# A gated cross-attention kernel on one core: the context arrives in 32-row blocks that VectorE turns, and three engines' lists are reordered

## The reference, cut to what matters

```python
x = x + jnp.tanh(g_xattn[0]) * xattn(layernorm(x), ctx, ctx, mask, W_q, b_q, W_k, b_k, W_v, b_v, W_o, b_o)
x = x + jnp.tanh(g_ffn[0]) * ffn(layernorm(x), gate_w, w1, w2)
# xattn, x and ctx are (4, 512, 256); 16 heads of 16; windows of 64 queries that see
# their own and the previous 64 keys, causal:
q, k, v = query @ W_q.T + b_q, ctx @ W_k.T + b_k, ctx @ W_v.T + b_v
attn = softmax(where(causal & valid & mask, q k^T / 4, lowest)); out = (attn v) @ W_o.T + b_o
# ffn: top-1 router over 16 experts, 160 places each; gelu(tokens @ w1[e]) @ w2[e], weighted
```

## Time and profile before

| | |
|---|---|
| median of 3 runs | 324.27 us (322.58 to 327.51) |
| the profiled execution | 323.56 us, its span in the trace 321.8 us |
| busy, share of the span | PE 93%, DVE 61%, ACT 55%, POOL 51% |
| attention of four batches | to about 165 us |
| transition and experts | 165 us to the end |

### The profile page before, as it was taken

The page is one execution under the profiler, slowest core; times in us unless marked ns, Lnnn a source line. Parts: engine busy times, 40 slices in busy tenths (PEclk is TensorE's granted clock), DMA queues, the critical chain, the costliest instruction groups (busy, mean ns, idle before and its releaser), DMA issues.

```text
span 321.8 us, 8449 instructions
## 1 busy us (share of the span) xinstructions
PE 300.3 (93%) x2759; PEld 245.3 (76%) x2760; DVE 195.4 (61%) x950; ACT 177.1 (55%) x666; POOL 165.5 (51%) x201
## 2 busy tenths in 40 slices
PE   7869879999999999999899999999999999999994
PEld 3438746887758866777788788888988989898974
DVE  2888898898999879899974331423325161515133
ACT  3479999999999999999755111111110202111110
POOL 6379647789769974989857112131313121121222
PEclk9997999999999999999999999999999999999999
DMA  7921299017512290230324689598979797997900
GB/s 217 280 95 25 81 378 298 5 26 239 189 67 91 58 305 3 94 86 9 92 98 182 173 234 353 171 364 255 365 226 368 216 367 245 310 305 246 373 20 13
DMA packets 48471, 60.55 MB, mean 188 GB/s; under 512 B 14712, under 2 KB 41360, under 8 KB 46384
## 3 DMA queue, kind: packets, MB, share of 16 engines
q1 hardware_dynamic: 44976, 53.20, 51.6%
q0 software_dynamic: 2560, 6.25, 5.3%
q10 hardware_dynamic: 896, 0.61, 0.6%
HBM read 44.60 MB, written 14.19 MB: 183 GB/s over the span
## 4 chain that ended last, share of the span: by engine, by line
PE 50%; ACT 26%; DVE 9%; issue 6%; DMA 4%; SPq 3%; POOL 1%; POOLq 0%; DVEq 0%; ACTq 0%
ACT probs L714 18%; PE bank L1765 18%; PE bank L1790 14%; PE bank L1815 4%; PE bank L1426 3%; ACT probsT L727 3%; DVE probs L960 3%; DMA w<-in_L_ffn_w_dram 2%; ACT q_par L688 2%; SPq L331 2%; PE bank L1437 2%; PE bank L1539 2%; PE bank L1479 1%; DMA x_all<-in_x_dram 1%; PE bank L1501 1%
## 5 line engine op out<-in xcount | busy, mean ns | idle before, releaser
L714 ACT ACTIVATE probs<-probs,low 128x128 f32<-128x128 f32 x256 | 99.3, 404 | 2.2 <-DVE low L960 2.2
L535 POOL TENSOR_TENSOR probs<-probs,r_total 128x512 f32<-128x512 f32 x64 | 66.4, 1047 | 18.4 <-DVE r_total L969 18.0
L1765 PEld LDWEIGHTS bank<-xdT,w 128*128 128x128 f32 x480 | 66.5, 190 | 2.8 <-issue 2.2
L1765 PE MATMUL bank<-xdT,w 128*128 128x160 f32 x480 | 68.0, 300 | 0.6 <-issue 0.4
L960 DVE CUSTOM_DVE_ANT_0 probs<-bank,mask_now 128x128 f32<-128x128 f32 x256 | 57.2, 283 | 7.6 <-PE bank L1467 7.2
L714 ACT ACTIVATION_READ_ACCUMULATOR probs<-probs,low 128x1 f32 x256 | 52.4, 205 | 0.0
L884 ACT ACTIVATE w_raw<-bank 128x480 f32<-128x480 f32 (+1 forms) x24 | 12.6, 526 | 61.4 <-PE bank L1765 57.6
L639 POOL DMA_INDIRECT out_dram<-base,place x16 | 14.0, 875 | 59.0 <-DVE base L1325 38.2
L648 POOL DMA_INDIRECT out_dram<-base,place x16 | 15.7, 980 | 53.8 <-DVE place L1318 43.6
L884 ACT ACTIVATE x_all<-bank 128x480 f32<-128x480 f32 (+1 forms) x24 | 12.6, 527 | 53.2 <-PE bank L1765 53.2
L1335 DVE SCALAR_TENSOR_TENSOR base<-bank,base 128x256 f32<-128x256 f32 x15 | 7.2, 482 | 51.7 <-PE bank L1790 51.6
(11 more groups left out here) (148 smaller groups left out, 495.4 us busy)
## 6 DMA issues: line engine op xcount, KB each, us to landing
w<-in_L_ffn_w_dram SPq DMA_DIRECT2D x32, 1024.0 KB, 7.1
expert_queue<-empty_row SPq DMA_DIRECT2D x1, 5140.0 KB, 17.7
q_blocks<-expert_queue SPq DMA_DIRECT2D x62, 40.0 KB, 3.0
base<-expert_queue SPq DMA_DIRECT2D x16, 129.0 KB, 4.6
ctx_rows<-in_ctx_dram SPq DMA_DIRECT2D x4, 512.0 KB, 9.7
out_dram<-rows SPq DMA_DIRECT2D x4, 512.0 KB, 6.3
x_all<-in_x_dram SPq DMA_DIRECT2D x3, 512.0 KB, 7.7
v_shift<-v SPq DMA_DIRECT2D x12, 128.0 KB, 2.3
```

The costliest lines, as they stand in the source:

```text
L535: pool.tensor_tensor(probs[:, i % NP_], probs[:, i % NP_], r_total[:, i % NP_].unsqueeze(2).to_broadcast([P, PAIRS, 2 * WINDOW]), ALU.mult ...
L714: last = act.activation(probs[:, i % NP_, j], probs[:, i % NP_, j], ACT.Exp, scale=-1.0, bias=low[:, i % NP_, j:j + 1], accum_out=total[:, ...
L1765: last = pe.matmul(ps_hidden[m][:, c * CAP:(c + 1) * CAP], w1_sb[i % 2][:, k, f * P:(f + 1) * P], xdT[i % 2][:, k], start=(k == 0), stop=( ...
```

## The change

- The tile `ctx_rows` becomes `ctx_blocks`, of the same size. For batch 0 it is still loaded as rows (`load_first_ctx`) and turned by PE (`first_ctxT_of`).
- For batches 1 to 3 `load_ctx(n)` issues four transfers. Each takes a quarter of the columns (64 of them, 256 bytes) of all 512 rows, as 16 blocks of 32 rows, into 32 partitions. It waits for `ctxT_turned` instead of `ctxT_ready`, and stands at the end of SP's list of a batch instead of at its start (`load_ctx(1)` stands right ahead of the loop, as before in effect).
- DVE turns the blocks straight into `ctxT` with two STREAM_TRANSPOSE of 512 elements for each partition (`turn_ctx(b + 1, 0)` and `(b + 1, 1)`), behind `take_v(b, 1)`. `ctxT_of` on PE and `take_ctxT` on ACT are gone for these batches. `ctxT` now holds even columns in its first half and odd ones in its second, so `wT_of` turns W_k and W_v, and `first_ctxT_of` batch 0's context, with a column step of two.
- The lists of PE, ACT, DVE and POOL get a new order within each batch and in the last one. `turn_queued_xd`, the first turn of queued rows, moves from the start of the expert stage into the last batch, ahead of `rank_of(LAST - 1)`.

```diff
-        ctx_rows = sb("ctx_rows", [P, T, D])
+        ctx_blocks = sb("ctx_blocks", [P, S // BLOCK, KD * BLOCK])
+        first_ctx = ctx_blocks[:].rearrange("p s c -> p (s c)").rearrange("p (t d) -> p t d", d=D)
...
             def load_ctx(n):
-                if n > 0:
-                    sp.wait_ge(ctxT_ready, value(n - 1, 2, 2))
-                sp.dma_start(ctx_rows[:], ctx_in[n].rearrange("(t p) d -> p t d", p=P)).then_inc(ctx_in_s, 16)
+                if not 0 <= n < B:
+                    return
+                if n == 1:
+                    sp.wait_ge(ctxT_ready, 2)
+                else:
+                    sp.wait_ge(ctxT_turned, value(n - 2, 2, 2))
+                for j in range(P // BLOCK):
+                    sp.dma_start(ctx_blocks[j * BLOCK:(j + 1) * BLOCK],
+                                 ctx_in[n, :, j * KD * BLOCK:(j + 1) * KD * BLOCK].rearrange("(s r) c -> r s c", r=BLOCK)
+                                 ).then_inc(ctx_in_s, 16)
...
+            load_ctx(1)
             for b in range(B):
-                if b < LAST:
-                    load_ctx(b + 1)
                 shift_v(b, 0)
...
                 if b > 0:
                     store_x1(b - 1)
+                load_ctx(b + 2)
...
+            def turn_ctx(n, half):
+                if not 0 <= n < B:
+                    return
+                dve.wait_ge(ctx_in_s, 16 + 16 * (P // BLOCK) * n)
+
+                dve.wait_ge(v_ready, value(n - 1, 2, 2))
+                blocks = slice(half * (S // BLOCK // 2), (half + 1) * (S // BLOCK // 2))
+                dve.transpose(ctxT[:, :, half * (S // 2):(half + 1) * (S // 2)].rearrange("p k (s r) -> p s k r", r=BLOCK),
+                              ctx_blocks[:, blocks].rearrange("p s (r k) -> p s k r", k=KD)).then_inc(ctxT_turned, 1)
...
-                pe.wait_ge(ctxT_taken, value(n, 2, 2))
+                if n == 0:
+                    pe.wait_ge(ctxT_taken, 2)
+                else:
+                    pe.wait_ge(ctxT_turned, value(n - 1, 2, 2))
```

More of the change, by code:

```diff
@@ L348, in _ @@
             load_x(0, T // 2, T, x_in_late)
-            load_ctx(0)
+            load_first_ctx()
             for i, b in enumerate((b_q, b_k)):
@@ L603, in _ @@
             norm(LAST, 1)
+            x1_norm(LAST - 1, 0)
             scatter(LAST - 2, 2)
             norm(LAST, 2)
-            scatter(LAST - 2, 3)
             norm(LAST, 3)
             norm(LAST, 4)
-            x1_norm(LAST - 1, 0)
+            x1_norm(LAST - 1, 1)
+            scatter(LAST - 2, 3)
             norm(LAST, 5)
-            x1_norm(LAST - 1, 1)
-            x1_rstd_of(LAST - 1, 1)
             norm(LAST, 6)
@@ L615, in _ @@
             norm(LAST, 8)
+            x1_rstd_of(LAST - 1, 1)
+            norm(LAST, 9)
+            norm(LAST, 10)
             x1_norm(LAST - 1, 2)
-            norm(LAST, 9)
-            x1_norm(LAST - 1, 3)
-            norm(LAST, 10)
             norm(LAST, 11)
@@ L624, in _ @@
             norm(LAST, 15)
+            x1_norm(LAST - 1, 3)
             x1_rstd_of(LAST, 0)
             scatter(LAST - 1, 0)
+            scatter(LAST - 1, 1)
             x1_rstd_of(LAST, 1)
-            scatter(LAST - 1, 1)
             x1_rstd_of(LAST, 2)
@@ L690, in take_q @@
                 last.then_inc(q_taken, 1)
[L692 to L698, removed]
             def take_k(n, g, ps):
@@ L805, in _ @@
                 exp(b, 5)
-                take_probsT(b, 1)
                 exp(b, 6)
                 exp(b, 7)
+                take_probsT(b, 1)
                 take_xnT(b + 1, 0, ps_misc)
+                exp(b, 8)
                 take_probsT(b, 3)
+                exp(b, 9)
                 take_x1nT(b - 1, 0)
[L812 to L816, removed]
                 take_xnT(b + 1, 1, ps_misc)
@@ L1242, in _ @@
             low_of(LAST, 7)
+            take_v(LAST, 0, ps_misc)
             take_probsT(LAST, 0)
-            take_v(LAST, 0, ps_misc)
             r_total_of(LAST, 4)
@@ L1296, in turn_queued_xd @@
-            def turn_queued_xd():
-                dve.wait_ge(rows_in[0], 16 * (P // BLOCK))
-                turn_rows(0).then_inc(queued_turned, 1)
             def take_first_xd():
@@ L1370, in pair @@
                     take_y(e + 1, i + 1)
-            turn_queued_xd()
             take_first_xd()
@@ L1593, in _ @@
             for k in range(KD):
-                ctxT_of(0, k, bank[k])
+                first_ctxT_of(k, bank[k])
             keep_warm(bank[3], 3)
@@ L1620, in _ @@
                 probsT_of(b, 0)
-                probsT_of(b, 1)
                 scores(b, 2)
@@ L1636, in _ @@
                 v_of(b, 1, ps_misc)
+                probsT_of(b, 4)
+                probsT_of(b, 5)
+                pe.wait_ge(v_taken, value(b, 2, 2))
+                xnT_of(b + 1, 1, ps_misc)
+                scores(b, 3)
+                pe.wait_ge(xnT_taken, value(b + 1, 2, 2))
+                x1nT_or_gate(b - 1, ps_misc)
                 if first:
@@ L1659, in _ @@
                 q_of(b + 1, 0, ps_misc)
+                probsT_of(b, 7)
                 if not first:
@@ L1696, in _ @@
             probsT_of(LAST - 1, 15)
-            probsT_of(LAST, 0)
             pe.wait_ge(q_taken, value(LAST, 2, 2))
@@ L1701, in _ @@
             attend(LAST - 1, 3)
+            probsT_of(LAST, 0)
+            probsT_of(LAST, 1)
             scores(LAST, 2)
-            probsT_of(LAST, 1)
             probsT_of(LAST, 2)
```

177 lines of the change are left out of this document (88 added, 89 removed).

## The result

The changed kernel takes 325.34 us in the median of 10 runs (323.93 to 326.67); beside it, the kernel before took 323.41 us in the median of 10 (322.58 to 327.51). The ratio is 1.0051, with an interval of 1.0031 to 1.0071: half a per cent slower, which is 1.6 us (1.0 to 2.3). The interval is far narrower than the 2% that the prediction took as the least that could be told. Forecast was 1.0% less, and 325.34 lies above the upper bound of 324.4. The profiled execution took 325.34 us with a span of 323.5, against 323.56 and 321.8.

The account below looks back on a forecast made before the run. ACT was taken to bound the first stage. Copies -2.9, idle ahead of them -0.5, xnT1 wait +0.5, take_q waits -0.5 and last batch +0.2 gave -3.2 us: 324.27 to 321.1 us, range 317.6 to 324.4.

Parts of the forecast that it names:

- What bounds the kernel: First stage, 35 to 146 us: ACT is fullest, about 36 of each 37 us, with the other engines close behind.
- What goes: ACT loses six context copies, 2.9 us, and 0.5 us idle ahead of them; PE loses transposes, 2.6 us.
- What comes: DVE gets two turns a batch at 0.65 us, 3.9 in all (2.6 to 4.2), covered by its idle time.
- rival 3: DVE becomes the bound: the turns' full 3.9 us are added and ACT's saving is worth nothing, 328.2 us; chance 0.06.
- (5): New order: norm and DVE collide in ways the order shifts, each worth 0.9 us either way; taken as none.
- (1) to (4): New order: later take_v makes ACT wait 0.5 us at xnT1; later norms and POOL steps hidden; take_q waits shrink 0.5.
- (6): Batch 0's context transposes and those of W_k and W_v read with a step of two; taken as zero.
- (7): turn_queued_xd moves into the last batch, where DVE is nearly full: cost 0 to 0.44 us, taken 0.2.
- The loads: Four smaller context transfers a batch cost nothing, hidden by 19 us of cover on SP; bytes some 26% longer.
- rival 4: Context blocks arrive late and the turn waits; fourfold occupation, 31 us, makes shift_v 4.4 late: 325.5 us; chance 0.03.
- The marks: First take_q of batches 1 to 3 starts 1, 2 and 3 us earlier; expert stage unchanged in length.
- Rival 2: ACT, freed, waits for DVE's low or PE's take_q; only some 0.5 us come back, 323.8 us; chance 0.19.

Follow-up runs that it names:

- e4: Kernel before, with the mask set for batch 0 alone and router weights of batches 0 to 2 written by a reciprocal without their factor: 324.35 us, ratio 0.9992.
- e10: Kernel before, with GpSimd writing the finished mask instead of DVE's mask operation: 323.66 us, ratio 0.9997.
- e13: e9 with each of the six turns done a second time into a spare tile that nothing reads: 324.64 us, 1.0050 of the kernel before.
- e1: Kernel before with the context in blocks and the turns alone, all engines keeping their old lists: 324.48 us, ratio 1.0010.
- e2: Changed kernel with its new loop, but the last batch's lists and turn_queued_xd in the old order: 326.57 us, 1.0083 of the kernel before.
- e6: Changed kernel with the mask set once, for batch 0 alone: 322.88 us, 0.9967 of the kernel before.
- e8: Changed kernel with two mask buffers, the mask set behind the second turn, and ACT multiplying the weights of batches 0 and 1: 323.09 us, 0.9968 of the kernel before.
- e9: Changed kernel with GpSimd writing the finished mask into three buffers, no mask operation on DVE: 322.62 us, 0.9968 of the kernel before.
- e5: Changed kernel with router weights of batches 0 to 2 written by a reciprocal, without their factor: 325.33 us, 1.0040 of the kernel before.
- e11: e1 (turns in the old order) with GpSimd writing the finished mask: 322.25 us, 0.9947 of the kernel before.
- e14: e11 with the changed kernel's lists for the last batch: 322.40 us, 0.9963 of the kernel before.
- e7: e1 with the mask set once and router weights of batches 0 to 2 written by a reciprocal, without their factor: 323.51 us, 0.9978 of the kernel before.

## Why the prediction was wrong

**What bounds the kernel.** Right as far as it went: ACT bounded the first stage, and what it saves is time until the next engine is full. e4 and e10 confirm the other side: DVE's 1.3 us of mask operations were worth nothing that can be told.

**What goes, What comes.** The prices held: the turn took 675 ns and holds DVE for 0.60 (taken: 0.65), and was never waited for. The step that failed is the sentence on the cover: "DVE's idle time in the three windows is 37 minus its busy time", of which 1.3 was to be covered and 1.8 to 3.7 left. The turns were booked at nothing; e13 puts them at up to 0.74 of their length, which for 3.6 us is 2.7. The sum with that term is -3.4 + 2.7 = -0.7 before the smaller terms; e1 measured +0.3 (0.0 to 0.7). No run accounts for the 1.0 between them; e1's profile holds 1.2 us more of DVE than the turns (+4.8 for 3.6), most of it `marks` operations beside GpSimd. The idle time of an engine in a chain of five is not a store to be drawn on: DVE's 5.0 us of waits for scores fell to 1.1, while ACT's for `q` rose from 2.2 to 4.1. That a step put into the chain delays what stands behind it, even when the engine has a gap some steps later, is how I read this; the runs show the price and not the path.

The prediction said as much in one sentence, "if that cover were gone, the 1.3 would count in full", and made it rival 3 at a chance of 0.06 with 328.2. The mechanism was the right one, its size too large: the turns count for part of their length, and ACT's saving keeps a worth (with all of the 3.6 us counting and no saving, e1 would stand at +3.6, and it stands at +0.3). POOL's waits for DVE's reciprocals, the row named against it, are no evidence either way: 16.8 us before and 17.4 after.

**The new order, (5).** "Each such accident is worth 0.9 us either way; I take none." The collisions were seen in the rows ahead of the change, and priced as luck with a mean of zero. This is the second term that failed: the loop's new order measured +2.4 us (e2 against e1) where it was booked at nothing. In the changed kernel four lie in batches 1 and 2 and hold 4.83 us where the same operations held 0.97 before. Of these, the mask operation's part is shown, together with the meeting of `seen` and `past` that goes when it goes: e6, e8 and e9 remove or move it in three ways, and each gains 0.83 to 0.84%. The profiles of e2 and e5, which share the loop, have the mask's row at 1.58 and 1.64 us in the same place, so it isn't the luck of one execution; with DVE the late engine it counts. That the mask operation would change places with `r13` the prediction doesn't mention. That (1) to (4) and (6) have no price is consistent with e9 and e11; none of them was tried alone.

**(7) and the last batch.** Taken as +0.2, bounds of 1 either way. Shown: -0.3% behind the new loop (e2 against the change, on the edge of its uncertainty), nothing behind the old one (e14).

**The loads.** Right: hidden. SP's occupation rose 1.9-fold. The limit of 2.5 that the prediction gave for it was miscounted: from 38.52 to 65.52 there is room for 27.0 us, 3.4 times 7.86, as its own rival 4 has it. The bytes were estimated at 26% longer; from the first issue to the last landing the three contexts took 9.9, 19.1 and 12.6 us, where they had taken 9.1, 18.5 and 10.3: 9, 3 and 22% more.

**The marks.** `take_q` was to start earlier by 1, 2 and 3 us; measured 1.5, 1.9 and 1.2. The first two batches followed the forecast, and the gain was given back by the end of the third. ACT's waits grew by 1.9 us in one line alone, and its idle time in the three windows from 3.1 to 6.7 us, more than the 3.4 that it had saved: the prediction's own sign of failure. The expert stage was to keep its length; it didn't quite. From the timelines, against the profile of before:

```
us against before         last exp   5th expert   6th expert to the end
change                     +1.57       +0.42       +1.61
e9                         -1.50       -2.83       -1.25
e11                        -1.97       -2.30       -1.50
e1                         -0.48       +0.03       +0.75
e10                        -0.45       +0.80       +0.80
e4                         -0.25       +0.14       +0.14
```

In the first four some 0.7 to 1.6 us are lost around the sixth expert's weights, whatever the sign of what came before; it is where a lead of 2.8 us becomes 1.3. e10, without turns, loses 1.1 one expert earlier and e4 nothing there, so the loss doesn't belong to the turns. Which transfer it is and why is open; no run was aimed at it. At the end of the first stage the two controls are 0.45 and 0.25 us ahead: the mask operation was worth little before, rather than nothing. Open as well: why e7 stays behind e11, and how the 1.3 us between e1 and the change divide between the mask's extra 1.1 us, `seen` and `past`, and the rest.

**Range and chances.** The range, 317.6 to 324.4, left out all that lay above the kernel before by more than nothing: the one rival on the slow side stood at 0.06, while the forecast's largest term was a cover that no row had tested. Rival 2, "ACT, freed, arrives early and waits", came nearest, with 323.8, and missed what the new order adds. Its row is the one seen: ACT waits for `low` (1.3 us) and `take_q` (4.1).

## What to carry to other kernels

When work moves from the fullest engine to the second fullest, don't book the second one's idle time as cover; look at who waits for it, and book the moved work at a good part of its length (here 0.6 to 0.7). Whether waits of the engine directly behind the place where it enters would hide it, no run here tried. Before such a swap look for cheap work to take off the receiving engine: here the mask's operation was worth nothing that could be told before the swap (e10) and 2.0 us after it (e11), and swap and mask together beat both kernels (0.9947). In a list with a new order, look up where VectorE's copies and tensor-scalar operations now fall against GpSimd's instructions; a four-element one can cost 1.5 us, and one that stands ahead of the next batch's first step can pass it on.

## What the runs showed of the hardware

- A DVE operation on four elements for each partition took 1.52 us beside two instructions of GpSimd and 0.23 us in the kernel before; a mask operation of 1024 elements 1.58 against 0.40. When the first of two such neighbours was changed into a reciprocal, the second one took 1.43 us instead of 0.16 (e5).
- The turn of 512 elements for each partition took 0.60 us from start to start, against 0.44 for 320: 0.16 us for 192 elements more. By that line 0.17 of the 0.44 us would be fixed, an estimate from two points.
- Four loads of 128 KB in pieces of 256 bytes, queued behind the 5.1 MB of empty rows, occupied SP for 14.86 us; one load of 512 KB in pieces of 1 KB had taken 7.86 at the same place. They landed 19.1 and 18.5 us after the first issue.
- With the six turns on DVE, 0.57 to 0.71 of a change in DVE's busy time showed in the kernel's time, by the estimate above (e9, e11, e13); in the kernel before, 1.1 us less of it showed at most 0.65 (e4).
